# Layer 3 of a four-layer network: gate/up products issued ahead of down products, with single tiles at both ends

## What is computed

```python
def _qdot(x, w, out_dtype=BF16):
    return jnp.dot(x.astype(E4M3), w.astype(E4M3), preferred_element_type=out_dtype)
ff_gate = _qdot(x, w_gating[0])
gate_value = jax.nn.gelu(ff_gate)
ff1 = _qdot(x, w_gating[1])
activations = gate_value * ff1
outputs = _qdot(activations, w_linear)
```

## Time and profile before

| | us |
|---|---|
| median of 3 runs | 520.41 (519.27 to 520.88) |
| profiled execution | 519.72 |
| its span in the trace | 517.8 |

### The profile page before, as it was taken

How to read it: one execution, slowest core, us unless ns; L and a number is a source line. 1 busy time by engine, 2 the same in 40 slices (tenths; PEclk the granted TensorE clock), 3 DMA queues, 4 the chain that set the end, 5 groups by cost and what they waited for, 6 DMA issues and landing times.

```text
span 517.8 us, 5641 instructions
## 1 busy us (share of the span) xinstructions
PE 437.8 (85%) x2006; PEld 269.3 (52%) x2006; DVE 377.9 (73%) x663; ACT 195.2 (38%) x339; POOL 108.0 (21%) x65
## 2 busy tenths in 40 slices
PE   0796789987670899999999999999999999987572
PEld 0342444776470377899998997534434434322120
DVE  4999888797899798768666686375566773347975
ACT  4450155652221486321544824250010030146481
POOL 0000000000000297322000000047466654350000
PEclk9998788998965599999999999899999999999695
DMA  7910000710192127744754239020000000000001
GB/s 294 416 48 1 1 0 0 288 69 1 43 327 76 44 53 234 236 130 162 203 184 160 85 128 332 6 84 0 0 0 1 1 0 0 0 0 1 1 26 55
DMA packets 12093, 47.76 MB, mean 92 GB/s; under 512 B 2866, under 2 KB 5147, under 8 KB 9763
## 3 DMA queue, kind: packets, MB, share of 16 engines
q1 hardware_dynamic: 10914, 43.48, 24.0%
q0 software_dynamic: 1152, 3.93, 3.1%
HBM read 45.04 MB, written 2.37 MB: 92 GB/s over the span
## 4 chain that ended last, share of the span: by engine, by line
PE 69%; DVE 22%; issue 3%; ACT 3%; DMA 3%; SPq 0%; DVEq 0%
PE bank L1417 9%; PE bank L1391 8%; PE bank L1506 7%; PE bank L1515 7%; PE bank L1426 5%; PE bank L1543 3%; PE bank L1546 3%; PE bank L1279 3%; DMA const<-in_const 3%; PE bank L1321 2%; PE bank L1340 1%; PE bank L1311 1%; PE bank L1482 1%; DVE arena L903 1%; PE bank L1383 1%
## 5 line engine op out<-in xcount | busy, mean ns | idle before, releaser
L568 ACT ACTIVATE early<-bank 128x512 f32<-128x512 f32 (+1 forms) x24 | 14.3, 596 | 98.5 <-PE bank L1515 90.4
L1133 DVE TENSOR_TENSOR early<-early,bank 128x512 f32<-128x512 f32 (+1 forms) x24 | 16.4, 684 | 48.0 <-ACT early L568 47.6
L1391 PE MATMUL bank<-onehot,rows 128*128 128x512 f32 x192 | 51.4, 406 | 0.0
L341 POOL DMA_INDIRECT arena<-token_rows,arena x24 | 35.6, 1484 | 70.4 <-DVE arena L921 36.9
L1417 PEld LDWEIGHTS bank<-arena 128*96 128x96 f32 x512 | 44.2, 165 | 4.0 <-issue 3.9
L1506 PE MATMUL bank<-cT,arena 128*128 128x512 f32 (+1 forms) x96 | 46.2, 606 | 0.0
L1515 PE MATMUL bank<-arena 128*128 128x512 f32 (+1 forms) x96 | 45.8, 596 | 0.1
L1417 PE MATMUL bank<-arena 128*96 128x48 f32 x512 | 44.8, 248 | 0.3 <-issue 0.3
L1391 PEld LDWEIGHTS bank<-onehot,rows 128*128 128x128 f32 x192 | 33.9, 189 | 6.1 <-DVE onehot L952 0.3
L354 POOL TENSOR_TENSOR early<-early,arena 128x512 f32<-128x512 f32 (+1 forms) x12 | 28.0, 2333 | 41.8 <-DVE early L1133 41.8
L352 POOL TENSOR_TENSOR early<-early,arena 128x512 f32<-128x512 f32 (+1 forms) x12 | 15.1, 1262 | 103.0 <-DMA arena<-pair_weights 98.1
(11 more groups left out here) (315 smaller groups left out, 869.2 us busy)
## 6 DMA issues: line engine op xcount, KB each, us to landing
arena<-in_w_gate SPq DMA_DIRECT2D x8, 768.0 KB, 4.8
arena<-in_w_up SPq DMA_DIRECT2D x8, 768.0 KB, 7.8
arena<-in_w_down SPq DMA_DIRECT2D x8, 768.0 KB, 9.5
const<-in_const SPq DMA_DIRECT2D x1, 2122.5 KB, 13.1
arena<-in_wq SPq DMA_DIRECT2D x1, 2048.0 KB
arena<-in_wo SPq DMA_DIRECT2D x1, 2048.0 KB, 9.3
kT<-in_kT SPq DMA_DIRECT2D x2, 512.0 KB, 5.3
xT<-in_xT SPq DMA_DIRECT2D x1, 1024.0 KB, 8.5
```

What stands on the lines that cost most here:

```text
L341: g.indirect_dma_start(xg[:, t % XRING, :], None, scratch[:, :], bass.IndirectOffsetOnAxis(ap=toki[:, t:t + 1].bitcast(U32), axis=0)).then ...
L1391: return mm(bank[2 * ct + ch][:], rows1[:, i % RRING, part, ct * P:(ct + 1) * P], onehot1[:, t, ch * CHUNK:(ch + 1) * CHUNK], start=False, ...
```

## The change

PE's list: `gu3(1)` moves ahead of `down2(10)`, `gu3(2)` ahead of `down2(11)`, `gu3(4)` and `gu3(5)` ahead of `bias_down2(1)`, and from then on both tiles of a pair two pairs on stand ahead of `down3`. New idle products (`idle3`: 6, 4 and 2, whose results nobody reads) wait for ACT's last copy and stand ahead of the last two `down3` and within the last. ACT's list: tile 0's two copies move ahead of the last SiLU of layer 2, `gate3(1)` from before tile 4 to before tile 6, and the copies of the first chunk's result from behind tile 9 to behind tile 11. DVE's list: pairs 0 and 7 are done as two single tiles each, `masked_down(1)` moves from behind pair 0 to behind pair 1, and `add2(1)` and `cond3(1)` stand behind pair 2.

```diff
--- before.py
+++ after.py
@@ -414,6 +414,16 @@
                 cc = slice(ch * CHUNK, (ch + 1) * CHUNK)
                 act.wait_ge(S("x3_ready"), 2 * ch + 2)
                 s.activation(cT[:, :, cc], xT[:, :, cc], ACT.Sigmoid).then_inc(S("sig3_ready"), 1)
+
+            def gate_up3(it):
+                pair, h = divmod(it, 2)
+                act.wait_ge(S("gu3_done"), it + 1)
+                if it >= 2:
+                    act.wait_ge(S("gelu3"), it - 1)
+                s.copy(g3[h], bank[2 * h][:]).then_inc(S("g3_ready"), 1)
+                if pair >= 2:
+                    act.wait_ge(S("prod3"), pair - 1)
+                s.copy(u3[pair % 2][:, h, :], bank[2 * h + 1][:]).then_inc(S("u3_ready"), 1)
 
             act.wait_ge(S("vec_cond_in"), 32)
             step(s.activation(dw[:], vecs[:, V_W:V_W + 8], ACT.Exp))
@@ -562,6 +572,8 @@
                 su, t1, c1, t2, c2, mix = l2bufs(it)
                 bu = bank[2 * (it % 2)]
                 for k in range(2):
+                    if it == NCH * H2T - 1 and k:
+                        gate_up3(0)
                     act.wait_ge(S(("first2_done", "second2_done")[k]), it + 1)
                     if 2 * it + k >= 1:
                         act.wait_ge(S("h2_ready"), 2 * it + k)
@@ -579,18 +591,13 @@
 
             for it in range(NCH * F3T):
                 pair, h = divmod(it, 2)
-                if it == 4:
+                if it == 6:
                     gate3(1)
-                act.wait_ge(S("gu3_done"), it + 1)
-                if it >= 2:
-                    act.wait_ge(S("gelu3"), it - 1)
-                s.copy(g3[h], bank[2 * h][:]).then_inc(S("g3_ready"), 1)
-                if pair >= 2:
-                    act.wait_ge(S("prod3"), pair - 1)
-                s.copy(u3[pair % 2][:, h, :], bank[2 * h + 1][:]).then_inc(S("u3_ready"), 1)
+                if it:
+                    gate_up3(it)
                 act.wait_ge(S("g3_ready"), it + 1)
                 s.activation(gg3[pair % 2][:, h, :], g3[h], ACT.Gelu_apprx_tanh).then_inc(S("gelu3"), 1)
-                if it % F3T == 1 and it >= F3T:
+                if it == F3T + 3:
                     for ct in range(CT):
                         act.wait_ge(S("down3_done"), F3T // 2)
                         s.copy(y3[ct], bank[6 + ct][:]).then_inc(S("y3_ready"), 1)
@@ -1170,23 +1177,43 @@
                         dve.wait_ge(S(f"stored{ct}"), 16)
                     v.tensor_tensor(r3[ct], xT[:, ct, ch * CHUNK:(ch + 1) * CHUNK], y3[ct], ALU.add).then_inc(S("out_ready"), 1)
 
-            for pair in range(NCH * F3T // 2):
-                dve.wait_ge(S("gelu3"), 2 * pair + 2)
-                dve.wait_ge(S("u3_ready"), 2 * pair + 2)
-                v.tensor_tensor(a3, gg3[pair % 2], u3[pair % 2], ALU.mult).then_inc(S("prod3"), 1)
-                dve.wait_ge(S("prod3"), pair + 1)
-                step(v.tensor_scalar(a3, a3, E4_TOP, 1.0 / E4_TOP, ALU.mult, ALU.mult))
-                step(v.tensor_scalar(e3.bitcast(I16), a3.bitcast(I16), 0x7F80, None, ALU.bitwise_and))
-                step(v.tensor_scalar(e3, e3, E4_MIN, 24.0, ALU.max, ALU.mult))
-                step(v.tensor_tensor(a3, a3, e3, ALU.add))
+            LAST = NCH * F3T // 2 - 1
+
+            def hidden3(pair, h):
+
+                one = slice(h, h + 1) if h < 2 else slice(0, 2)
+                a, e, q = a3[:, one, :], e3[:, one, :], q3[pair % 2][:, one, :]
+                dve.wait_ge(S("gelu3"), 2 * pair + min(h, 1) + 1)
+                dve.wait_ge(S("u3_ready"), 2 * pair + min(h, 1) + 1)
+                first = v.tensor_tensor(a, gg3[pair % 2][:, one, :], u3[pair % 2][:, one, :], ALU.mult)
+                if h:
+                    first.then_inc(S("prod3"), 1)
+                    dve.wait_ge(S("prod3"), pair + 1)
+                else:
+                    step(first)
+                step(v.tensor_scalar(a, a, E4_TOP, 1.0 / E4_TOP, ALU.mult, ALU.mult))
+                step(v.tensor_scalar(e.bitcast(I16), a.bitcast(I16), 0x7F80, None, ALU.bitwise_and))
+                step(v.tensor_scalar(e, e, E4_MIN, 24.0, ALU.max, ALU.mult))
+                step(v.tensor_tensor(a, a, e, ALU.add))
                 if pair >= 2:
                     dve.wait_ge(S("down3_done"), pair - 1)
-                v.tensor_tensor(q3[pair % 2], a3, e3, ALU.subtract).then_inc(S("q3_ready"), 1)
-                dve.wait_ge(S("q3_ready"), pair + 1)
-                if pair == 0:
+                last = v.tensor_tensor(q, a, e, ALU.subtract)
+                if h or pair == LAST:
+                    last.then_inc(S("q3_ready"), 1)
+                    dve.wait_ge(S("q3_ready"), pair + 1 + (h == 1 and pair == LAST))
+                else:
+                    step(last)
+
+            for pair in range(NCH * F3T // 2):
+                if pair in (0, LAST):
+                    hidden3(pair, 0)
+                    hidden3(pair, 1)
+                else:
+                    hidden3(pair, 2)
+                if pair == 1:
                     masked_down(1)
+                if pair == 2:
                     add2(1)
-                if pair == 1:
                     cond3(1, 0)
                     cond3(1, 1)
                     cond3(1, 2)
@@ -1566,6 +1593,12 @@
                         last = mm(bk[:], wg3[:, ct, o_ + f * P:o_ + (f + 1) * P], c8[:, ct, cc], start=(ct == 0), stop=(ct == CT - 1))
                 last.then_inc(S("gu3_done"), 1)
 
+            def idle3(n):
+
+                pe.wait_ge(S("u3_ready"), NCH * F3T)
+                for _ in range(n):
+                    mm(bank[0][:], wl3[:, 0, 0:P], c8[:, 0, 0:CHUNK], start=True, stop=True)
+
             def down3(pair):
                 ch, p = divmod(pair, F3T // 2)
                 pe.wait_ge(S("q3_ready"), pair + 1)
@@ -1575,6 +1608,9 @@
                     pe.wait_ge(S("dm2_ready"), 2)
                 for h in range(2):
                     f = 2 * p + h
+                    if h and pair == NCH * F3T // 2 - 1:
+                        idle3(2)
+                        pe.wait_ge(S("q3_ready"), pair + 2)
                     for ct in range(CT):
                         last = mm(bank[6 - 2 * ch + ct][:], wl3[:, f, ct * P:(ct + 1) * P], q3[pair % 2][:, h, :],
                                   start=(f == 0), stop=(f == F3T - 1))
@@ -1637,18 +1673,22 @@
             pe.wait_ge(S("w3_ready"), 1)
             gu3(0)
             gu2(NI - 1, 1)
+            gu3(1)
             down2(NI - 2)
-            gu3(1)
+            gu3(2)
             down2(NI - 1)
-            gu3(2)
             gu3(3)
+            gu3(4)
+            gu3(5)
             bias_down2(1)
-            for pair in range(NCH * F3T // 2):
+            down3(0)
+            for pair in range(1, NCH * F3T // 2):
                 if 2 * pair + 4 < NCH * F3T:
                     gu3(2 * pair + 4)
+                    gu3(2 * pair + 5)
+                else:
+                    idle3(6 if pair == NCH * F3T // 2 - 2 else 4)
                 down3(pair)
-                if 2 * pair + 5 < NCH * F3T:
-                    gu3(2 * pair + 5)
 
 
 def constants():
```

## The result

The changed kernel is slower, as forecast: 524.38 us (median of 7 runs) against 520.03 us for the kernel before, run beside it. The ratio is 1.0099, with a 95% interval of 1.0072 to 1.0126. Now and then an execution of any of these kernels takes about 2% longer at a lower granted clock (530.68 us once for the kernel before), and such executions are left out of all ratios. The forecast was 524.7 us. The profiled execution took 523.30 us with a span of 521.2, which is 3.4 us above the span of before.

The account below looks back on a forecast made before the run. DVE sets the pace from 466.35 to the end. Start 3.5 us sooner, splits +2.3, old waits of 5.2 gone, new waits 11.9, tail -1.3: +4.2 (+4.3 by ACT's copy), so 524.7 us, range 523.4 to 526.1.

Parts of the forecast that it names:

- Start and pair 1: Start of layer 3: first split done early, then DVE waits 3.5 to 6 us for gu3(3); pair 1 starts at 473.45.
- The clock at `bias_down2(1)`: After 5.1 us of PE idle time the clock is at half level; bias_down2(1) takes 3.73 us for four.
- the wait for `down3(0)`: DVE's last operation of pair 2 overwrites the buffer down3(0) reads, so it waits 2.35 us.
- Rival 1: Clock stays full through both new PE pauses: 3.7 us less in all, +0.6 or 521.0 us; chance 0.08.
- Sigmoid and `c8`: Between add2(1) and cond3(1) nothing covers the sigmoid: 1.2 us idle; hand-over to PE at 493.9, 8.7 us late.
- The wait for tile 9: After pair 3, gu3(8) and gu3(9) run at half clock, so DVE waits 1.85 us for the GELU.
- the wait of 0.5 for pair 5: DVE waits 0.5 us for tile 11 before pair 5, in place of 1.33; clock back by gu3(10).
- +4.3 forecast for the stretch: Layer 3 up to ACT's last copy, which starts at 517.0 instead of 512.64: +4.3 us.
- Single tiles and tail: Last pair: 2.36 us a tile, 1.16 more in all; DVE's end to ACT's copy 0.7 us, giving back 1.28.
- Rival 2: Single tiles cost DVE as much as pairs: last pair 2.4 us more, 527.1 us; chance 0.08.
- A side estimate of the prediction: Split of the last pair: with the skill's 58-cycle fixed term it would cost about 0.4 us less.
- rival 3: Idle products fail to keep the clock up: last half of down3(7) at 1.2 GHz, +0.45, 525.2 us; chance 0.14.

Follow-up runs that it names:

- Run 2: Changed kernel with masked_down(1) behind pair 0 again, all else as changed: ratio 0.9997 to the kernel before, layer 3 stretch 50.98 us.
- Run 3: Changed kernel with idle products filling PE's pauses before bias_down2(1) (18) and gu3(8) (22): ratio 1.0047 to the kernel before.
- run 5: Changed kernel with masked_down(1) behind pair 0, add2(1) behind pair 1, cond3(1) behind pair 2: ratio 0.9963 to the kernel before.
- run 1: Kernel before with only the change's end: last pair as two tiles, down3(7) in halves, the idle products: ratio 0.9993.
- run 9: Changed kernel without its twelve idle products, split of the last pair kept: ratio 1.0068 to the kernel before.
- run 7: Kernel of run 6 plus 33 idle products between down3(1) and gu3(8): 515.87 us, ratio 0.9926 to the kernel before.
- 10: The changed kernel itself again, run beside the second try with pair 0 whole: ratio 1.0089 to the kernel before.
- 4: Changed kernel's PE and ACT orders, with DVE's list of before and no idle products: ratio 0.9972 to the kernel before.
- 8: Changed kernel with pair 0 whole on DVE, first try: ratio 1.0068 to the kernel before.
- 11: Changed kernel with pair 0 whole on DVE, second try, beside the changed kernel: ratio 1.0055 to the kernel before.
- 6: Kernel of run 5 with gu3(1), gu3(2) behind down2(10), down2(11) again and pair 0 whole: ratio 0.9962 to the kernel before.
- 12: Kernel of run 7 plus two idle fp32 products in PE's pause before gu3(0): 515.69 us, ratio 0.9924 to the kernel before.

## Why the prediction was right

*Start and pair 1.* Forecast 473.45 for the start of pair 1, measured 473.41. Run 2 showed that the wait before it is where the loss begins: with `masked_down(1)` in it, 4.2 us came back, the 4.2 I had written down for that run. The length of that wait was forecast at 6.0 us and is 4.90, because the second single tile took 3.27 us and not 2.36 (see the last section). It cost nothing, since pair 1 starts when tile 3 is there.

*The clock at `bias_down2(1)`.* Forecast half level and 3.73 us, measured 0.50 and 3.78; the wait for `down3(0)` 2.35 forecast, 2.37 measured. That they agree to 0.02 us is luck in part: DVE got there 0.15 us sooner than forecast, and the wait ended 0.13 sooner. Run 3 showed the link by keeping the clock up. It was 2.1 us of that wait and 1.0 of the one for tile 9. Rival 1, the clock staying at its full level, did not come by itself; its price of 3.7 us was 3.0 when I forced it. Most of the difference is the 0.5 for pair 5 (below), which was not there to be won.

*Sigmoid and `c8`.* 1.2 forecast, 1.12 measured; `c8` at 493.9 forecast, 493.65 measured.

*After it.* The wait for tile 9 was 1.85 and is 1.84. The term that was mis-sized is the wait of 0.5 for pair 5: it is 0. The clock was back at 496.9, 3.3 us after PE had taken up `gu3(8)`, and `down3(2)` ran at the full level, so both tiles for pair 5 were ready. I had read 4.9 us for that return off one place of the kernel before. It is a term that comes and goes: in run 5 the clock was back 5.9 us after `gu3(8)` (mean 0.64 from 493 to 494), `down3(2)` was still slow and the wait was there, 0.88 us. This and the 0.25 at `c8` are nearly all of the difference between +4.3 forecast for the stretch and +3.4 measured.

*Single tiles and tail.* 2.36 us a tile forecast, 2.36 measured for both tiles of the last pair (the terms that were added up for it give 2.33); the two operations that I had placed between bounds take 0.42 and 0.29 us, as interpolated from the earlier trace rows. Rival 2 is refuted. The tail is 0.71 where I had 0.7, and run 1 shows that split and tail together are -0.1 us, as I had it (the other half of its 0.26 is a GELU wait). A side estimate of the prediction, that a smaller fixed part would make the split about 0.4 us cheaper, comes to 0.5 by its own terms, with six more instructions; the sum does not use it.

*The idle products* (rival 3) did keep the clock up in the changed kernel; run 9 prices them at 0.4 us, where I had 0.45. They do not do so always: of the eleven profiles with these twelve idle products, the last two products took 0.60 or 0.61 us in nine, 0.94 in run 5 and 1.01 in run 7. In both the clock fell just after PE had paused for 1.32 us, a length that I had called shorter than any that lowered it.

*The median.* The ratio of 1.0099 is 5.1 us of 520.0, and the stretch gives 3.4. Two executions of the changed kernel, 527.65 and 527.94 us, are nearly 4 us longer than the other five; without them the mean difference is 4.1 us. The rest stays open: the interval begins at 1.0072, which is 3.7 us, and no trace shows a place for more in the changed code. So it is partly luck that the measured median of 524.38 comes within 0.3 us of the forecast 524.7. The walk gave 0.9 us too much for layer 3, and the executions took longer than layer 3 accounts for. What the runs bear out is the mechanism and a loss of 3.4 us.

## What to carry to other kernels

When one engine's list is rewritten, write the lists of the engines that feed it anew as well: here PE's and ACT's new orders were worth -1.5 us by themselves and became +3.4 us because DVE's pieces had been put behind too many pairs. A piece that another engine waits for (`masked_down(1)`) belongs into the first wait of its own engine that is long enough, and independent work belongs between a request and its answer (pair 2 between `add2(1)` and `cond3(1)`). A split tile costs its fixed part at every instruction (0.42 us for half the columns here, where the whole takes 0.69) and gains only where something waits for the half.

## What the runs showed of the hardware that was not expected

**One pause, two outcomes.** PE's pause before `gu3(0)` is 2.23 us in all kernels but the last (2.44 in the trace of run 9, which lacks one record there). In ten of these thirteen profiles the clock stayed at 1.00, and in three (runs 1, 3 and 5) it fell. From run 1, PE's row behind the pause, DVE's last gate product, and the clock:

```profile
457.76 1.86 PE L1586 MATMUL bank<-wkv_a,arena 128*128 128x512 bf16 x4 [2.23 <-issue]
...
462.88 0.68 DVE L1133 TENSOR_TENSOR early<-early,bank 64x512 f32<-64x512 f32 x1 [4.63 <-ACT early L568]
...
458.00:459.00 1.00, 1.00 (x4) 0.50 0.00 0
```

`gu3(0)` takes 1.86 us instead of 1.02 and the last gate product waits 4.63 us instead of 3.05. The same instructions in the same order thus differ by 1.6 us from one execution to the next, which is as much as several of the edits here are worth. It is why the stretch inside layer 3 is the steadier measure.

**DVE beside POOL.** In the changed kernel one operation of the second single tile takes three times as long as its like:

```profile
466.37 1.40 POOL L358 TENSOR_TENSOR early<-early 64x512 f32<-64x512 f32 x1 [3.41 <-PE bank L1573]
...
466.69 1.36 DVE L1197 TENSOR_TENSOR ekT<-ekT 128x512 bf16<-128x512 bf16 x1
```

The DVE operation lasts 1.36 us where the same one takes 0.43 in the first tile (464.33) and 0.42 in the last pair (514.56). Both engines end within 0.3 us of each other. The same pairing stands in the profiles of runs 2, 3, 5, 9 and 10 with 1.37 us. Where pair 0 is whole and PE has the new order (runs 4, 8 and 11), the same operation of 1024 columns takes 1.63 or 1.64 us instead of 0.69. In the five profiles with PE's old order (the kernel before and runs 1, 6, 7 and 12) the POOL operation is over before pair 0 begins, and the DVE operation takes 0.69 us as usual. The Trainium skill says in "GPSIMD Engine Reference", in its table of specifications, that the SBUF interfaces are shared with VectorE; the traces agree as far as the lengthening goes. It cost nothing: it lay in the wait for tile 3 or, in runs 2, 4 and 5, ahead of a wait of 1.88 or 2.29 us that PE ends.
